# Four seams of a gated cross-attention block on one core: early loads, compact last keys, one weight block, output projection two tiles ahead

## What is computed

```
def ternarize(W):
    delta = 0.05 * max(abs(W)); mask = abs(W) > delta
    alpha = sum(where(mask, abs(W), 0)) / max(sum(mask), 1)
    return alpha * sign(W) * mask
q = rms_norm(layernorm(x) @ w_q.T + b_q, g_q)
k_img, v_img from context[:, :257]; k, v from context[:, 257:]
att = attention(q, k, v, mask) + attention(q, k_img, v_img)
x = x + tanh(g_xattn) * (att @ w_o.T + b_o)
h = gelu(layernorm(x) @ ternarize(W1).T + b1)
y = h @ ternarize(W2).T + b2
x = x + tanh(g_ffn) * fp4(y)     # one scale from max(abs(y))
```

## Time and profile before

| | |
|---|---|
| median of 3 runs | 3434.43 us (3434.35 to 3438.99) |
| the profiled execution's own time | 3427.94 us |
| its span | 3425.6 us |
| TensorE busy | 3069.4 us, 90% |
| VectorE busy | 2112.4 us, 62% |
| ScalarE busy | 1567.9 us, 46% |
| GpSimd busy | 1377.3 us, 40% |
| mean granted TensorE clock | 0.948 of full speed |

### The profile page before, as it was taken

One profiled execution on the slowest core, in us unless ns is written; L12 is line 12 of the kernel. 1 busy time (PEld: TensorE's weight loads), 2 busy tenths in 40 slices (PEclk: granted clock), 3 DMA queues, 4 the chain that ended last, 5 costly groups with the idle time before them and its releaser, 6 DMA issues. The chain is left out here.

```text
span 3425.6 us, 49995 instructions
## 1 busy us (share of the span) xinstructions
PE 3069.4 (90%) x15756; PEld 1893.1 (55%) x15756; DVE 2112.4 (62%) x3591; ACT 1567.9 (46%) x2973; POOL 1377.3 (40%) x547
## 2 busy tenths in 40 slices
PE   6999999997699999999999999999991388999991
PEld 5777777786344444444444444444430266777771
DVE  4667676664566666666676666676635785443435
ACT  3444344433166666666665666666660153222222
POOL 0000000000268778777787787687780062000000
PEclk8999999998699999999999999999995599999996
DMA  4666666668655645645645646556513162000005
GB/s 147 170 166 165 168 164 166 163 170 130 138 104 118 130 102 123 125 101 125 127 98 124 126 99 128 121 103 130 103 36 109 45 201 68 1 1 0 0 1 196
DMA packets 366642, 384.72 MB, mean 112 GB/s; under 512 B 41137, under 2 KB 291057, under 8 KB 359801
## 3 DMA queue, kind: packets, MB, share of 16 engines
q1 hardware_dynamic: 355080, 323.61, 39.6%
q0 software_dynamic: 7168, 50.34, 8.6%
q10 hardware_dynamic: 4224, 8.39, 0.6%
HBM read 210.77 MB, written 121.15 MB: 97 GB/s over the span
## 5 line engine op out<-in xcount | busy, mean ns | idle before, releaser
L915 ACT ACTIVATE at_probs<-at_st 128x512 f32<-128x512 f32 (+1 forms) x1664 | 913.6, 595 | 630.6 <-PE at_st L765 619.7
L945 DVE TENSOR_REDUCE at_cm<-at_mx 128x2 f32<-128x896 f32 x768 | 813.0, 1086 | 449.8 <-PE at_mx L781 449.8
L725 POOL TENSOR_TENSOR at_added<-at_added,at_probs 128x2048 f32<-128x2048 f32 x192 | 888.5, 4627 | 11.5
L765 PE MATMUL at_st<-at_qst,at_kst 101*128 101x512 f32 (+1 forms) x1664 | 657.4, 457 | 4.1 <-ACT at_probs L915 3.7
L765 PEld LDWEIGHTS at_st<-at_qst,at_kst 101*128 101x128 f32 (+1 forms) x1664 | 266.2, 185 | 597.7 <-ACT at_probs L915 450.1
L781 PE MATMUL at_mx<-at_kst,at_qst 97*128 97x448 f32 (+1 forms) x2048 | 531.1, 362 | 57.1 <-DMA at_kst<-stack_rows 30.3
L803 PE MATMUL at_acc<-at_probs,at_vt 128*32 128x512 f32 (+2 forms) x3584 | 485.3, 606 | 5.8 <-issue 4.9
L781 PEld LDWEIGHTS at_mx<-at_kst,at_qst 97*128 97x128 f32 x2048 | 372.1, 194 | 165.8 <-DVE at_cm L945 77.4
L693 POOL MEMSET at_ones<- 128x32 f32 x1 | 0.1, 129 | 826.3 <-POOLq L262 826.3
L725 POOL TENSOR_TENSOR at_added<-at_probs 128x2048 f32<-128x2048 f32 x32 | 146.4, 4576 | 341.4 <-ACT at_probs L915 341.4
L1390 ACT ACTIVATE ff_h<-ff_psa,ff_b1c,alpha 128x512 f32<-128x512 f32 x128 | 99.5, 778 | 344.5 <-PE ff_psa L1367 344.5
(11 more groups left out here) (202 smaller groups left out, 4731.8 us busy)
## 6 DMA issues: line engine op xcount, KB each, us to landing
at_kst<-k_high SPq DMA_DIRECT2D x256, 200.1 KB
at_probs<-at_probs POOLq DMA_DIRECT2D x32, 1024.0 KB, 7.0
at_kst<-k_low SPq DMA_DIRECT2D x128, 200.1 KB
pj_xin<-in_ctx_dram SPq DMA_DIRECT2D x96, 256.0 KB, 4.1
k_high<-pj_kh SPq DMA_DIRECT2D x96, 256.0 KB, 3.2
k_low<-pj_kl SPq DMA_DIRECT2D x96, 256.0 KB, 4.7
values<-pj_vs SPq DMA_DIRECT2D x96, 256.0 KB, 4.5
at_vt<-values SPq DMA_DIRECT2D x32, 768.0 KB
```

The source lines that it names most:

```text
L725: pool.tensor_tensor(added[:], so_far, probs[:, SLOT[t]], ALU.add).then_inc(S["add_done"], 1)
L765: pe.matmul(st[0:kn, h % 2, :], kst[g.j][:, h, t * P:t * P + kn], qst[g.j][:, h, :], start=True, stop=True).then_inc(S["st_done"], 1)
L915: act.activation(probs[0:kn, SLOT[t], h, :], st[0:kn, h % 2, :], ACT.Exp, scale=SCALE).then_inc(S["exp_done"], 1)
L945: dve.tensor_reduce(dst, mx[:, 2 * slot:2 * slot + 2, 0:kn], AX.X, ALU.max, negate=last).then_inc(S["mx_free"], 1)
```

## The change

Projection: the first three context loads and the constants are issued in the block that prepares the weights, by a new `Started`. The tables of live keys are built after the first tile, the mask row after the eleventh, and the stack rows are stored at the thirteenth. The tile of last image keys and three of the four left-over tiles stand before the last batch, and one left-over tile after it. The last keys go to scratch arrays of their own with two stores, and each group of attention reads its column from there with three small loads.

Weights: `ternarize` and the preparation of `w_o` become one block. Loads come in pieces of 1 MB. VectorE works on pieces of 2048 columns in two passes; the sum for alpha comes from two Relu passes on ScalarE (the weights beyond the threshold), plus count times threshold. ScalarE does all evacuations. `ident` is kept from the start. The raw weights lie in `xy`, which is free then.

Output projection: three buffers for each part, low parts two tiles ahead on GpSimd, ScalarE's high part ahead of its root, and the last small step as a tensor_scalar.

```diff
+        self.x_ready = [a.sem(f"x_ready{p}") for p in range(4)]
+        self.const_in = a.sem("const_in")
+    def load(self, sp):
+        for n, (_, kind, idx) in enumerate(ORDER[:AHEAD]):
+            k0 = idx * P if kind == "img" else NIMG + idx * P
+            sp.dma_start(self.xin[n][:], self.ctx_in[0, k0:k0 + P, :]).then_inc(self.x_ready[n], 16)
+        for t in ("img", "txt", "q"):
+            sp.dma_start(self.bias[t][:], self.rows["b_" + t].partition_broadcast(P)).then_inc(self.const_in, 16)
+            sp.dma_start(self.gain[t][:], self.rows["g_" + t].partition_broadcast(P)).then_inc(self.const_in, 16)
...
-ENDING = [("extra", 0)] + [("rem", k) for k in range(4)]
+BETWEEN = [("extra", 0), ("rem", 0), ("rem", 1), ("rem", 2)]
+ORDER = [(i, kind, idx) for i in range(B - 1) for kind, idx in SEQ]
+ORDER += [(None, kind, idx) for kind, idx in BETWEEN]
+ORDER += [(B - 1, kind, idx) for kind, idx in SEQ] + [(None, "rem", 3)]
...
                 if kind == "extra":
-                    for c in range(NG):
-                        out_k(khv[:, :, c, SK - 1].rearrange("b d -> d b").bitcast(F32), h3[:, c, 0:B], allow_slow_non_contiguous=True)
-                        out_k(klv[:, :, c, SK - 1].rearrange("b d -> d b").bitcast(F32), l3[:, c, 0:B], allow_slow_non_contiguous=True)
+                    out_k(kxh_d.rearrange("c d b -> d c b").bitcast(F32), h3[:, :, 0:B])
+                    out_k(kxl_d.rearrange("c d b -> d c b").bitcast(F32), l3[:, :, 0:B])
...
+            for n in range(len(ORDER)):
+                step(Token(0, n))
+                if n == AUX_AT:
+                    sp.wait_ge(S["aux_set"], 6)
+                    for r in range(2):
+                        sp.dma_start(aux_d.rearrange("(b r) s k -> r b s k", r=2)[r], aux[:]).then_inc(S["aux_out"], 16)
...
+                for r, d in enumerate((kxh_d, kxh_d, kxl_d)):
+                    sp.dma_start(kst[p][r * HD:(r + 1) * HD, :, SK - 1:SK].bitcast(F32),
+                                 d[G % NG, :, G // NG:G // NG + 1].bitcast(F32).rearrange("(h d) b -> d h b", d=HD),
+                                 allow_slow_non_contiguous=True).then_inc(q_in[p], 16)
...
-                    pe.wait_ge(q_in[w.j], 48 * (w.i + 1))
+                    pe.wait_ge(q_in[w.j], 96 * (w.i + 1))
...
-        oh, ol = (some(n, 2, [P, D], F32R) for n in ("oh", "ol"))
+        oh, ol = (some(n, 3, [P, D], F32R) for n in ("oh", "ol"))
...
             low_o(0)
+            low_o(1)
             pool.wait_ge(S["bo_done"], 1)
             for n in range(N):
                 with_bias(n)
-                if n + 1 < N:
-                    low_o(n + 1)
+                if n + 2 < N:
+                    low_o(n + 2)
...
             for n in range(N):
-                root(n)
                 if n + 2 < N:
                     high_o(n + 2)
+                root(n)
                 normalize(n)
...
-                dve.scalar_tensor_tensor(l[:, 8:9], l[:, 4:5], -1.0, l[:, 6:7], ALU.mult, ALU.mult).then_inc(S["step"], 1)
+                dve.tensor_scalar(l[:, 8:9], l[:, 6:7], -1.0, l[:, 4:5], ALU.mult, ALU.mult).then_inc(S["step"], 1)
...
+            load(0)
+            sp.dma_start(nato[:], w_o.rearrange("(o p) i -> p o i", p=P)).then_inc(o_in, 16)
+            load(1)
...
+            for s in range(4):
+                largest(0, s)
+            row_largest(0)
+            threshold(0)
+            three_levels(0, 0)
+            three_levels(0, 1)
+            largest(1, 0)
+            largest(1, 1)
+            three_levels(0, 2)
+            three_levels(0, 3)
+            largest(1, 2)
+            largest(1, 3)
+            row_largest(1)
+            for c in range(NG):
+                low_weights(c)
+            threshold(1)
+            for s in range(4):
+                three_levels(1, s)
...
+                for r, sign in enumerate((1.0, -1.0)):
+                    if 2 * n + r >= 2:
+                        act.wait_ge(S["over_done"], 2 * n + r - 1)
+                    act.activation(over[r][:], piece(w, s), ACT.Relu, bias=m[:, w, 3:4], scale=sign,
+                                   accum_out=sums[:, w, 2 + r, s:s + 1]).then_inc(S["over_done"], 1)
...
+            for s in range(4):
+                beyond(1, s)
+                if s:
+                    evacuate(1, s - 1)
+            evacuate(1, 3)
```

More of the change, by code:

```diff
@@ L216, in __init__ @@
         if not self.real:
             return
[L218 to L233 removed]
+        self.k, self.p, self.x4 = k, k % 2, k % 4
@@ new lines, in __init__ @@
+        if known:
+            self.i, self.kind, self.idx = ORDER[self.n]
+            earlier = ORDER[:self.n]
+            self.vn = sum(kind != "q" for _, kind, _ in earlier)
+            self.vp = self.vn % 2
+            values = [kind for _, kind, _ in ORDER if kind != "q"]
+            ready = sum(LOADS.get(kind, 1) for n, (_, kind, _) in enumerate(ORDER[:self.n + 1]) if n % 4 == self.x4)
+            self.x_ready = 16 * ready
+            self.k_before = 16 * sum(K_STORES.get(kind, 2) for n, (_, kind, _) in enumerate(earlier) if n % 2 == self.p)
+            self.v_before = 16 * sum(V_STORES.get(kind, 1) for n, kind in enumerate(values[:self.vn]) if n % 2 == self.vp)
+            self.k_stored = self.k_before + 16 * K_STORES.get(self.kind, 2)
+            self.v_stored = self.v_before + 16 * V_STORES.get(self.kind, 1)
+            return
@@ L235, in at @@
+        self.i = i
+        self.kind, self.idx = SEQ[k]
+        vk = sum(kind != "q" for kind, _ in SEQ[:k])
+        self.vn, self.vp = NVAL * i + vk, vk % 2
+        self.x_ready = 16 * ((NSEQ // 4) * i + k // 4 + 1)
+        self.k_before = 32 * ((NSEQ // 2) * i + k // 2)
+        self.v_before = 16 * ((NVAL // 2) * i + vk // 2)
     def at(self, step):
+        if isinstance(self.n, int):
+            return Token(0, self.n + step)
         return Token(self.i, self.k + step)
@@ L263, in project @@
         a = Names(nc, ctx, "pj")
-        xin = [a.sb(f"xin{p}", [P, D]) for p in range(4)]
+        xin, bias, gain, len_i, klen_i = started.xin, started.bias, started.gain, started.len_i, started.klen_i
         xh = [a.sb(f"xh{p}", [P, D], F32R) for p in range(2)]
@@ L402, in turn_x @@
             def turn_x(t):
-                pe.wait_ge(x_ready[t.x4], 16 * (t.round + (2 if t.kind == "rem" else 1)))
+                pe.wait_ge(x_ready[t.x4], t.x_ready)
                 if not early(t.n, 2):
@@ L1229, in _, with dst @@
+        piece = lambda w, s: nat[:, 16 * w + 4 * s:16 * w + 4 * s + 4, :]
+        PIECES = [(w, s) for w in range(2) for s in range(4)]
+        bank_of = lambda w, s, half: 8 * w + 2 * s + half + (4 if w else 0)
+        def dst(w, s, half):
+            if w == 0:
+                return t1[:, 2 * half:2 * half + 2, s * D:(s + 1) * D]
+            return t2[:, 4 * s + 2 * half:4 * s + 2 * half + 2, :]
         @block.sync
         def _(sp):
-            sp.dma_start(nat[0][:], srcs[0]).then_inc(w_in[0], 16)
@@ L1281, in _ @@
                 dve.reciprocal(m[:, w, 6:7], m[:, w, 5:6]).then_inc(S["a_step"], 1)
[L1282 to L1288 removed]
+                dve.wait_ge(S["a_step"], b + 5)
@@ new lines, in evacuate @@
+            def evacuate(w, s):
+                for half in range(2):
+                    k = bank_of(w, s, half)
+                    act.wait_ge(S["turned"], k + 1)
+                    act.activation(dst(w, s, half), ps[:, k % 8, :].bitcast(BF16).rearrange("p (r d) -> p r d", r=2),
+                                   ACT.Copy).then_inc(S["evacuated"], 1)
+            for s in range(4):
+                beyond(0, s)
+                if s:
+                    evacuate(0, s - 1)
+            evacuate(0, 3)
```

318 lines of the change are left out of this document (164 added, 154 removed).

## The result

The changed kernel takes **3350.11 us** (median of 4 runs, 3349.82 to 3351.22) where the kernel before, run beside it, takes 3436.26 (3434.35 to 3438.99): a ratio of 0.9754, 95% interval 0.9736 to 0.9772. The forecast was 3357 with a range of 3340 to 3374, and faster with 0.97. The span fell from 3425.6 to 3347.8, by 77.8 us; my sum said 77.1. The parts of the sum tell another story.

The account below looks back on a forecast made before the run. TensorE bounds most stages; gains lie where it idles: projection start and end, weights, output projection. Terms 12.5 + 11.6 − 1.5 + 52.5 + 2.0 = 77.1 us less give 3350.8; 6.5 more to the median makes 3357, range 3340 to 3374.

Parts of the forecast that it names:

- Start: Projection start: with context loads and constants issued early, the first product comes near 30.4 instead of 42.87, 12.5 us less.
- Tables "beside products, at nothing": Projection, VectorE: building tables behind the first and eleventh tile costs nothing beside TensorE's products; 3.3 us without that cover.
- The stack rows "have long landed": Projection end: their store, moved to the thirteenth tile, has landed well before the end; no cost was entered.
- Three remainder tiles in mid-stream: Projection: three left-over tiles with six stores each, now in a full stream, lose 1.5 us, bounds 0 and 5.1.
- Old tail: Projection end before the change: TensorE lost 5.1 us to late stores, all of it saved now.
- New tail: Last projection product to attention's first load: 11.1 us instead of 19.1, 8.0 saved.
- The rival that the moved tiles drain as badly as the old tail: Projection: that, or the early loads land late; 5 to 9 us less gained, 3364 in all; chance 0.07.
- Attention's start: Three more small loads in the first group delay attention's first product by 1.5 us, bounds 0.5 and 3.
- Its loop: Attention's later groups: loads are issued more than half a group ahead, so the small loads change nothing.
- Weights: Merged weight block: 72.5 us instead of 125.07, 52.5 less, with ScalarE setting the end; bounds 46 and 56.
- 4-byte reads: Rival, attention: TensorE waits for the small key loads in each of 32 groups; 3 us each gives 3453; chance 0.02.
- ring: Output projection: a two-tile dependency from residual through GpSimd's x with bias sets 3.92 us per tile; stage 2 us less.

Follow-up runs that it names:

- a2: The changed kernel with the two stores of the stack rows back behind the last store of the projection; ratio 0.9752 to the kernel before.
- a12: The changed kernel with the last image keys stored and read as in the kernel before, without attention's small loads; 3365.49 us, ratio 0.9774.
- a5: The changed kernel with GpSimd's x with bias ahead of the low part and the third small layer-norm step as a tensor_scalar; 3340.46 us, ratio 0.9706.
- a3: The changed kernel with only GpSimd's order turned round in the output projection, x with bias ahead of the low part; ratio 0.9751.
- a6: The changed kernel with the last small layer-norm step of the output projection as a scalar_tensor_tensor again; 3373.02 us, ratio 0.9796.
- b4: The kernel before with one more projection batch written out on TensorE alone, moving its attention loop by 976 instructions; 3426.36 us, ratio 0.9947.

## Why the prediction was right, and where it was not

The forecast of the total was right and its reasons were not all: two stages missed by 17 and 15 us in opposite directions.

**Start.** Right: 29.62 for 30.4, since the loads had landed and the first tile's steps were priced by rows.

**Tables "beside products, at nothing".** Failed. I reasoned from idle time in an average tile. VectorE runs in order: the tables stand ahead of the next split and bias addition, and each made a tile late, 9.82 − 8.07 = 1.75 and 6.24 − 4.47 = 1.77 us. I had named 3.3 us as the price without cover; it was 3.5, for there was none.

**The stack rows "have long landed".** Failed, by 7.7 us, the largest miss within the projection. I asked when they were needed and not what stood behind them, although SyncE issues four DMAs per tile in one queue, and a load that is late stops TensorE.

**Pace of the tile.** Not in the sum at all: 7.6 us, 4 to 6 of them by addresses. Nothing in the profile of before could show it.

**Three remainder tiles in mid-stream.** Taken as 1.5, bounds 0 and 5.1. From the 113th to the last tile takes 122.98 us; the batch before that took 96.93, so the four extra tiles took 26.05, 6.51 each: nothing lost. **Old tail**: 5.1 was too low, 8.05 (128.25 less a batch of 94.68 less four tiles of 6.38), since the last batch was disturbed too. **New tail**: right in size, 11.47 for 11.1, but not by what I named alone: I put the saving down to ScalarE's wait and the last values, and by a2 some 5 us of the 7.6 saved there are the stack rows, which the old tail stored last. The rival that the moved tiles drain as badly as the old tail fell; the compact stores alone were worth 7.2 (a12).

**Attention's start**: 0.5 for 1.5, and a12 says that even this isn't the loads. **Its loop**: "nothing" failed by 15.4 us, in my favour, 5 of them by the clock. My plan for it was sound (a changed pace would prove me wrong) but I never looked at the groups one by one in the kernel before, where every third is longer. That the written-out part of a loop moves all code behind it was no step of mine.

**Weights**: right by its own steps. The second threshold (47.9 for 48.2), the price of a piece on VectorE (4.66 us for 4.8) and of ScalarE's four rounds (23.3 for 24) held; the first threshold stood at 17.6 and not 16.7, and cheaper pieces made up for it. "VectorE having finished near 71" contradicts my own 67.4; it was 66.75. **4-byte reads**: in that rival's 2.2 us per group, 1.8 for three issues do not fit the 0.4 per issue stated elsewhere; with that it is 1.6. None of it showed.

**Output projection**: right, ring and all: period, last link, the 0.21 us step. The rival that TensorE would set the pace at 3.46 was wrong for this change, and right about who comes next: with the ring cut (a5) TensorE does set it, at 3.34. The rival that the stall stays did not come true either; a3 and a6 show that it moves to L1164 (L1214 there) as soon as something shifts.

**From span to median.** I added 6.5 us, the distance of the profiled run to the median before. Afterwards the median lies 0.3 above the profiled run and all runs within 1.4 us. Why the spread shrank is not shown. The stall at the jump back differs from one jump to the next, but b4, without it, still spread over 8.2 us (3419.01 to 3427.24), and a5 over 6.1. So 3357 was 7 too high though the sum hit the span; the true errors of the stages were 17 and 15.

## What to carry to other kernels

An instruction or a DMA that is moved costs what stands behind it in its queue, whatever the engine's idle share says: list the next three items of that queue. Unrolling or shortening a loop moves every later loop; where a loop is longer at its jump back, and "issue" stands before a matmul, shift the code by some instructions before anything else is tuned. Read the granted clock behind a stall, for here a stop of one to two microseconds cost as much again in clock. Beside a busy GpSimd, give VectorE's small steps a form that isn't held up, all of them, for the next one of the old form takes over the wait.

## What the runs showed of the hardware

A loop's place in the instruction stream was worth 13 to 30 us of 3400, and in the longest groups about half of it was the clock, granted at 0.50 for some 3 us behind the stop in the kernel before (from 1385) and 6 in the one with the transposes (from 1225). The addresses of the projection's buffers changed the spacing of 512-column matmuls by some 2% (0.229 us from start to start with the old ones, 0.233 with the new).

VectorE beside GpSimd: a scalar_tensor_tensor of one column ran until the end of GpSimd's tensor_tensor in the rows shown (0.72, 0.78, 0.84 and the earlier trace rows 0.96 us for 0.2), and a tensor_scalar of one column with one or two scalar columns did not (0.21, 0.27). So the stall that the prediction's second rival feared for the tensor_scalar did not come. Under GpSimd's memsets a cast of 8 columns and tensor_scalars of 10 did wait (2.30 us for 0.17), so the form alone does not make an operation safe. The Trainium skill, page "SBUF — State Buffer", section "SBUF: two separate sides", has two-input operations wait only for a GpSimd operation that reads SBUF. The tensor_tensor of 64x4 beside the memsets, the first half of the 2.03 us above, is no test of this, for it stood behind the tensor_scalars.
